# Layer 0's cross-attention: key norms spread through a row in DRAM, maxima of the two halves exchanged by two DMAs from ScalarE

## The reference, cut to what matters

```python
xn = layernorm(x, ln_x_g, ln_x_b)
ln = layernorm(latents, ln_l_g, ln_l_b)
q = (ln @ Wq).reshape(b, m, h, d).transpose(0, 2, 1, 3)
kv = jnp.concatenate([xn @ Wkv, ln @ Wkv], axis=1)
...
qn = rmsnorm(q, qn_g) * scale
kn = rmsnorm(k, kn_g)
sim = jnp.einsum('bhid,bhjd->bhij', qn, kn)
...
attn = jax.nn.softmax(sim.astype(jnp.float32), axis=-1).astype(sim.dtype)
out = jnp.einsum('bhij,bhjd->bhid', attn, v)
out = out.transpose(0, 2, 1, 3).reshape(b, m, h * d)
return out @ Wout + bout
```

## Time and profile before

| | us |
|---|---|
| median of 3 runs | 3336.15 |
| lowest and highest | 3332.85, 3337.33 |
| the profiled execution | 3327.6 |
| its span | 3325.8 |
| steps of the stage, first `shift` to last | 122.4 to 1313.0 |
| TensorE busy, whole span | 2892.9 (87%) |
| VectorE, ScalarE, GpSimd busy | 1606.0, 1071.9, 508.3 |

### The profile page before, as it was taken

One profiled execution on the slowest core, in us unless ns is written; L12 is line 12 of the kernel. 1 busy time (PEld: TensorE's weight loads), 2 busy tenths in 40 slices (PEclk: granted clock), 3 DMA queues, 4 the chain that ended last, 5 costly groups with the idle time before them and its releaser, 6 DMA issues. The chain is left out here.

```text
span 3325.8 us, 44201 instructions
## 1 busy us (share of the span) xinstructions
PE 2892.9 (87%) x17968; PEld 1930.7 (58%) x17968; DVE 1606.0 (48%) x3626; ACT 1071.9 (32%) x1925; POOL 508.3 (15%) x280
## 2 busy tenths in 40 slices
PE   4899999999999999779999978998965789688776
PEld 2465656666665666445555635666942459577644
DVE  4445454545555443535555546764531340355564
ACT  2232323333333322114445536532321423111121
POOL 2011120202020200000000004761010130243200
PEclk8899999999999999889999989998987889899898
DMA  4000000000000000121010001115857149423001
GB/s 135 0 1 22 1 23 6 18 23 1 23 1 23 1 1 1 71 106 41 21 41 21 1 6 33 45 41 203 320 195 229 50 163 324 146 86 113 32 1 32
DMA packets 80704, 215.92 MB, mean 65 GB/s; under 512 B 5232, under 2 KB 53896, under 8 KB 73848
## 3 DMA queue, kind: packets, MB, share of 16 engines
q1 hardware_dynamic: 77528, 204.98, 18.2%
q0 software_dynamic: 2976, 8.13, 0.7%
HBM read 201.99 MB, written 10.58 MB: 64 GB/s over the span
## 5 line engine op out<-in xcount | busy, mean ns | idle before, releaser
L1339 PE MATMUL L_xattn_bank<-L_xattn_keys_tok,L_xattn_probsT 119*128 119x257 f32 (+1 forms) x1792 | 437.6, 389 | 1.4 <-ACT L_xattn_probsT L1172 1.4
L1273 PE MATMUL L_xattn_wide<-L_xattn_keys_feat,weights_a 128*128 128x512 f32 (+2 forms) x1024 | 388.1, 523 | 3.0 <-DVE L_xattn_max L1008 1.3
L1339 PEld LDWEIGHTS L_xattn_bank<-L_xattn_keys_tok,L_xattn_probsT 119*128 119x128 f32 (+1 forms) x1792 | 324.3, 189 | 112.3 <-ACT L_xattn_probsT L1172 42.6
L1166 ACT ACTIVATE L_xattn_scores<-L_xattn_scores,L_xattn_neg_max 128x833 f32<-128x833 f32 x128 | 119.7, 983 | 627.7 <-DVE L_xattn_neg_max L1013 627.7
L1273 PEld LDWEIGHTS L_xattn_wide<-L_xattn_keys_feat,weights_a 128*128 128x128 f32 x1024 | 190.6, 192 | 157.7 <-issue 128.7
L2280 DVE TENSOR_TENSOR_SCAN L_attn_state<-L_attn_decay,L_attn_banks 128x1024 f32<-128x1024 f32 x80 | 182.7, 2286 | 69.6 <-PE L_attn_banks L2483 61.6
L998 DVE TENSOR_TENSOR L_xattn_k_normed<-L_xattn_wide,L_xattn_k_normed 128x834 f32<-128x834 f32 x128 | 125.4, 1021 | 172.8 <-PE L_xattn_wide L1287 172.8
L1555 DVE CUSTOM_DVE_ANT_0 L_xattn_scores<-L_xattn_banks,L_xattn_mask 128x512 f32<-128x512 f32 (+1 forms) x256 | 131.5, 570 | 151.8 <-issue 151.8
L1093 POOL TENSOR_TENSOR L_xattn_keys_tok<-L_xattn_keys_tok,weights_a 119x1792 f32<-119x1792 f32 (+2 forms) x24 | 61.1, 2545 | 938.4 <-DVE L_xattn_keys_tok L933 938.4
L2386 POOL TENSOR_TENSOR L_attn_state<-L_attn_state,L_attn_C_rows 128x1024 f32<-128x1024 f32 x80 | 188.7, 2360 | 70.3 <-DVE L_attn_state L2280 70.2
L1008 DVE CUSTOM_DVE_ANT_0 L_xattn_scores<-L_xattn_wide,L_xattn_mask_row 128x833 f32<-128x833 f32 x128 | 126.4, 1021 | 129.4 <-issue 129.4
(11 more groups left out here) (506 smaller groups left out, 4590.8 us busy)
## 6 DMA issues: line engine op xcount, KB each, us to landing
L_xattn_ctx_feat<-in_ctx_feat SPq DMA_DIRECT2D x24, 1601.0 KB, 10.2
L_ffn_expert_w<-in_x_L_ffn SPq DMA_DIRECT2D x16, 2056.0 KB, 8.4
L_ffn_expert_w<-in_x_L_ffn SPq DMA_DIRECT2D x15, 1028.0 KB, 6.0
L_ffn_expert_w<-in_x_L_ffn SPq DMA_DIRECT2D x15, 1024.0 KB, 5.6
L_xattn_keys_tok<-in_ctx_tok SPq DMA_DIRECT2D x8, 1547.0 KB
L_attn_C_rows<-L_attn_c_rows SPq DMA_DIRECT2D x48, 256.0 KB, 3.2
L_xattn_ctx_tok<-in_ctx_tok SPq DMA_DIRECT2D x8, 1536.0 KB
L_xattn_ctx_tok_and_one<-in_ctx_tok SPq DMA_DIRECT2D x8, 1536.0 KB
```

The source lines that it names most:

```text
L1273: last = nc.tensor.matmul(wide[:, 2 * h + c, 0:n], wk[:, k, p * P:(p + 1) * P], xnT[b % 2][:, k, a:a + n], start=(k == 0), stop=(k == KT - 1))
L1339: last = nc.tensor.matmul(bS[:, 0:D + 1], pT[0:r, c, a, :, :].rearrange("p h q -> p (h q)"), xn[b % 2][0:r, t, :], start=(t == 0), stop=(t ...
```

## The change

1. `spread` on TensorE is gone. ScalarE stores the norms of a step as rows into a small DRAM tensor `k_scale_rows` (two DMAs, four rows of 417 numbers each), and SyncE loads them back, each row broadcast to 64 partitions (two DMAs of 64 x 1668 numbers, 427 KB each), into the SBUF tile `spread`. `keys_normed` reads that tile, one iteration later than before, and `scores` waits for the clamp of step s + 1 in place of its product.
2. `swap_max` on TensorE is gone. ScalarE issues two DMAs of 64 x 2 numbers that move each half's maxima to the partitions of the other (`other`); `shift` becomes a maximum and a negation and moves into the iteration of its own scores, as do the exponentials.
3. TensorE's order: transposes of groups 0 and 1 between the two halves of the keys, groups 2 and 3 after them, the mix cut into 4, 2 and 8 tiles in place of 5, 5 and 4 (in an order that takes the tiles of ScalarE's copies first), `apply_v` behind the scores.
4. SyncE loads the tokens of a context as 112 and 7 partitions in place of 119, and from batch 2 on behind the norms' load of step p = 1. VectorE's statistics come after `shift`.

```diff
+    EVEN = 112
...
+    MIX_ORDER = [(c, a) for part in (range(4), range(4, HALF_T)) for c in range(2) for a in part]
...
+        spread = sb("k_scale", [P, 4, QK])
+        k_scale_rows = nc.dram_tensor(name + "k_scale_rows", (2, 2, KP), F32, kind="Internal").ap()
...
+        other = sb("max_of_other_half", [P, 2])
...
+                near = (TILES - 1) * TR
+
+                def load_ctx(b):
                     if b >= 2:
                         sp.wait_ge(mixed, NQ * (b - 1))
-                    near = (TILES - 1) * TR
                     rows = L.aps["ctx_tok"][b]
-                    sp.dma_start(xn[b % 2][0:TR, 0:TILES - 1, 0:D], rows[0:near, :].rearrange("(t p) d -> p t d", p=TR)
-                                 ).then_inc(ctx_loaded[b % 2], 16)
+                    far = rows[0:near, :].rearrange("(t p) d -> p t d", p=TR)
+                    for a, c in ((0, EVEN), (EVEN, TR)):
+                        sp.dma_start(xn[b % 2][a:c, 0:TILES - 1, 0:D], far[a:c]).then_inc(ctx_loaded[b % 2], 16)
...
+                def move_latents(b):
+                    sp.dma_start(xn[b % 2][NEAR:NEAR + S, TILES - 1, 0:D], L.z[(b % 2) * S:(b % 2 + 1) * S, b // 2, :]
+                                 ).then_inc(latents_moved[b % 2], 16)
+
+                def spread_scale(s):
+                    sp.wait_ge(k_scale_stored, 32 * (s + 1))
+                    if s >= 1:
+                        sp.wait_ge(kn_ready, 2 * s)
+                    for h in range(2):
+                        sp.dma_start(spread[h * DH:(h + 1) * DH, :, :].rearrange("p j n -> p (j n)"),
+                                     k_scale_rows[s % 2, h:h + 1, :].broadcast_to([DH, KP])).then_inc(k_scale_moved, 16)
+
+                load_ctx(0)
+                load_mask(0)
+                sp.wait_ge(latents_ready, 1)
+                for b in range(2):
+                    move_latents(b)
+                load_ctx(1)
+                load_mask(1)
+                for s in range(STEPS):
+                    b, p = divmod(s, NQ)
+                    spread_scale(s)
+                    if p == 1 and 1 <= b < B - 1:
+                        load_ctx(b + 1)
+                        move_latents(b + 1)
+                        load_mask(b + 1)
+
...
                     if piece == 0:
-                        dve.wait_ge(ctx_loaded[b % 2], 32 * (b // 2) + 32)
+                        dve.wait_ge(ctx_loaded[b % 2], 48 * (b // 2) + 48)
...
                 def keys_normed(s):
-                    dve.wait_ge(k_spread, s + 1)
+                    dve.wait_ge(k_scale_moved, 32 * (s + 1))
                     for x in range(2):
                         k = kn[:, s % 2, 2 * x * QK:2 * (x + 1) * QK].rearrange("p (a n) -> p a n", n=QK)
-                        nc.vector.tensor_tensor(k, wide[:, 2 * x:2 * x + 2, 0:QK], k, ALU.mult).then_inc(kn_ready, 1)
...
-                    dve.wait_ge(swapped, s + 1)
-                    nc.vector.scalar_tensor_tensor(nm[:, :], mx[:, :], -1.0, bO[:, 320:322], ALU.mult, ALU.min
-                                                   ).then_inc(shifted, 1)
+                    dve.wait_ge(swapped, 32 * (s + 1))
+                    chain(nc.vector.tensor_tensor(mx[:, :], mx[:, :], other[:, :], ALU.max))
...
-                    if behind:
-                        shift(s - 1)
                     if ahead:
                         key_copy(s + 1, 0)
+                    if behind:
+                        weights_turned(s - 1, 1)
+                    if ahead:
                         key_copy(s + 1, 1)
                     if behind:
-                        weights_turned(s - 1, 1)
                         weights_turned(s - 1, 3)
+                    if s < STEPS:
+                        keys_normed(s)
                     if ahead:
                         key_clamp(s + 1)
-                    if ahead:
-                        keys_normed(s + 1)
-                    if s >= 2:
-                        keep_result(s - 2)
                     if turns:
                         keys_turned(b + 1, p - 5, 0)
                     if s < STEPS:
                         score_max(s)
-                        if turns:
-                            keys_turned(b + 1, p - 5, 1)
-                        if b + 1 < B:
-                            if p == 1:
-                                ctx_stats(b + 1, 0)
-                            if p == 2:
-                                ctx_stats(b + 1, 1)
-                                ctx_norm(b + 1, 0)
-                            if p == 3:
-                                ctx_norm(b + 1, 1)
+                    if s >= 2:
+                        keep_result(s - 2)
+                    if s < STEPS:
+                        shift(s)
+                    if turns:
+                        keys_turned(b + 1, p - 5, 1)
+                    if s < STEPS and b + 1 < B:
+                        if p == 1:
+                            ctx_stats(b + 1, 0)
+                        if p == 2:
+                            ctx_stats(b + 1, 1)
+                            ctx_norm(b + 1, 0)
+                        if p == 3:
+                            ctx_norm(b + 1, 1)
...
+                    act.wait_ge(k_rnorm, 2 * s + 2)
+                    if s >= 2:
+                        act.wait_ge(k_scale_moved, 32 * (s - 1))
+                    for h in range(2):
+                        nc.scalar.dma_start(k_scale_rows[s % 2, h].rearrange("(j n) -> j n", n=QK), rk[h:P:32, :]
+                                            ).then_inc(k_scale_stored, 16)
+
+                def swap_max(s):
+                    act.wait_ge(s_taken, 2 * s + 2)
+                    if s >= 1:
+                        act.wait_ge(shifted, s)
+                    for c in range(2):
+                        nc.scalar.dma_start(other[(1 - c) * S:(2 - c) * S, :], mx[c * S:(c + 1) * S, :]).then_inc(swapped, 16)
...
                     if behind:
-                        exponentials(s - 1)
+                        weights_turned(s - 1, 0)
                     if ahead:
                         key_square(s + 1, 0)
                     if behind:
-                        weights_turned(s - 1, 0)
+                        weights_turned(s - 1, 2)
                     if ahead:
                         key_square(s + 1, 1)
-                    if behind:
-                        weights_turned(s - 1, 2)
                     if s >= 2:
                         mixed_turned(s - 2)
                     if ahead:
@@ -1208,6 +1253,9 @@
                     if turns:
                         keys_turned(b + 1, p - 5, 0)
                         keys_turned(b + 1, p - 5, 1)
+                    if s < STEPS:
+                        swap_max(s)
+                        exponentials(s)
...
-                    elif s:
+                    if s == 1 and h == 0:
+                        pe.wait_ge(k_clamped, 1)
+                    if s >= 2:
                         pe.wait_ge(s_taken, 2 * (s - 2) + h + 1)
...
-                def spread(s):
-                    pe.wait_ge(k_rnorm, 2 * s + 2)
-                    for j in range(4):
-                        last = nc.tensor.matmul(wide[:, j, 0:QK], L.const[32 * j:32 * (j + 1), C_SPREAD:C_SPREAD + P],
-                                                rk[32 * j:32 * (j + 1), :], start=True, stop=True)
-                    last.then_inc(k_spread, 1)
...
                     b, p = divmod(s, NQ)
-                    pe.wait_ge(kn_ready, 2 * min(s + 1, STEPS - 1) + 2)
-                    if s + 1 == STEPS:
+                    pe.wait_ge(kn_ready, 2 * s + 2)
+                    if s + 1 < STEPS:
+                        pe.wait_ge(k_clamped, s + 2)
...
-                    pe.wait_ge(s_taken, 2 * s + 2)
-                    if s >= 2:
-                        pe.wait_ge(att_ready, s - 1)
-                    nc.tensor.matmul(bO[:, 320:322], L.const[:, C_SWAP:C_SWAP + P], mx[:, :], start=True, stop=True
-                                     ).then_inc(swapped, 1)
-
...
-                        pe.wait_ge(pT_odd, 2 * s + 2)
                         if s >= 1:
                             pe.wait_ge(oh_ready, s)
-                    for t in tiles:
+                    if tiles[0] == 4:
+                        pe.wait_ge(pT_odd, 2 * s + 2)
...
                     pe.wait_ge(oh_ready, s + 1)
```

46 lines of the change are left out of this document (19 added, 27 removed).

## The result

The changed kernel takes 3488.57 us (median of 4 runs, 3478.69 to 3492.07) against 3334.5 (3332.34 to 3337.33) on the same chip: ratio 1.0457, 95% interval 1.0434 to 1.048. It is 154 us **slower**; 3270 was forecast, with 3228 to 3345 as the range.

What follows compares the result with a forecast made beforehand. TensorE's queue was taken as the bound; -74 + 25 - 6 - 9 = -64 gave 3263.6 from 3327.6 us, and with the runs' 8.5 us offset, rounded down, 3270 us. Range 3228 to 3345 us.

Steps and rivals of the forecast that it cites:

- the exchange, now a transfer: Maxima moved by two small ScalarE DMAs: landing L 3.3 us beside the norms' stream, stall 0.4 us a step, +25 us.
- Rival B: Exchange waits for the whole queued stream: L 4.4 us, stall 1.5 us, +93 instead of +25, 3340 us; chance 0.13.
- Rival C: Exchange lands like 128 KB transfers, L 5.7 us; TensorE stalls 2.8 us before each step's transposes; 3421 us; chance 0.11.
- Matmuls out of the step: TensorE's queue loses spread, exchange and a wait: -1.20 us a step, plain step 17.16, -74 us over 62 steps.
- The norms' round trip: Norms through DRAM land with 6 us of cover before VectorE's product; product reading SBUF within 0.2 us, covered; cost 0.
- Rival A: Exchange hidden, L under 2.9 us: no stall, and the statistics' 10 us gained; 3237 us; chance 0.32.
- Loading context 0: At the start, loading 112 and 7 partitions instead of 119 shortens VectorE's wait: -6 us, bounds 0 and -12.9.
- Ramp: Keys of step 1 and scores of step 0 start earlier, needing only clamps: -9 us, bounds -4 and -9.
- Statistics behind: VectorE's context statistics placed after the wait for the exchange: 2.6 us late in step 2, against 2.5 before; cost 0.

Runs made afterwards that it cites:

- experiment 9: Changed kernel, norms' loads issued three ways: four DMAs of 417 columns each, 3316.55 us; destination padded into short rows, 3531.5; second load after the first landed, 3328.19.
- the padded run: Changed kernel with the loads' destination padded by a column, so each partition gets four rows of 1668 bytes: 3531.5 us, ratio 1.0577.
- experiment 8: Changed kernel with 20, then 10, added matmuls filling TensorE's wait before the first transposes: 3564.44 us, then 3478.17 us.
- experiment 1: Changed kernel with SyncE issuing the norms' loads only when the exchange of the step before has landed: 3268.32 us, ratio 0.9805.
- experiment 6: experiment 1 with GpSimd's gain and bias done tile by tile: 3223.33 us, ratio 0.9667; the same edit in the kernel before: 3327.71 us.

## Why the prediction was wrong

**The step that failed** is *the exchange, now a transfer*: "If it shares each engine evenly with the stream it lands at the latest as the stream ends, L = 3.4. I take 3.3". There is no even sharing. L is 5.2 us and an issue 0.53 instead of 0.35; the stall was put at 0.4 us a step, +25, and is about 2.6 (19.62, the shortest plain step, less 17.01), over 62 steps +162. The end of the stream was also set too early, at S + 7.5: a 427 KB load takes 5.4 us here, and the second is issued near S + 3.6.

*The rivals.* Rival B had the right mechanism, waiting for everything queued, and the Trainium skill's packet rule beside it ("DMA: Bandwidth & Descriptors", on queues, rings and completion order). The changed kernel agrees with that rule, experiment 9 only in part: each load of the padded run has 16 rows an engine, 32 in both, more than the 9 to 17 after which the rule switches, and in the 25 steps with both loads ahead nearly everything still went first. B's price was off for the same reason as above, L = 4.4. Rival C had the sign, the place (`turn_weights(s, 0)`) and nearly the size, 2.8 us a step; it got 0.11. The row of 5.7 us was the only one of small transfers beside a stream, and I argued it away by the stream's size.

*A term that was missing.* The wait's effect on the clock. The sum priced a stall at its length; in a plain step in which the clock fell it costs some 1.5 us more (experiment 8). Of the 223 us between the stages of the changed kernel and of experiment 1, 66 are matmuls that ran slower, at 0.95 against 0.99 in the mean. C's 3421 comes within 68 us of 3489 without this term, but also without the products' loss and the stops told below, so that the two sizes are alike is partly luck.

*Matmuls out of the step*, -1.20 and a plain step of 17.16: right, 17.01 once the exchange is out of the way, and the wait before the first tile of the mix, read as forecast (from the mixed tokens' two transposes, less 0.23), is 0.29 us in the median (0.24 forecast).

*The norms' round trip*, 0 for its landing: right, 1.9 us of waiting in all. But "the product reads SBUF where it read PSUM; both bounds within 0.2 us, covered too" failed: beside GpSimd it takes up to 4.54 us. With what by-tile gains change in the ramp it was worth 45 us in experiment 1 (3268 to 3223), which is why Rival A's 3237 was missed there and beaten in experiment 6. In the changed kernel it is part of the third steps' 25.2 us. The prediction did not weigh this neighbour of the new operand.

*Loading context 0*, -6: the wait shrank by 6.1 us; made alone the edit gave 8.5, by its interval 5 to 15. *Ramp*, -9: together with the context -15, and the first scores start 11.5 us earlier, the first `shift` 11.3; in experiment 1 it is 16.4. *Statistics behind* `shift`, 0: off; in experiment 1 their place was worth 14 us.

*A second path through the exchange*, put at nothing. Once in a batch, in its seventh step, TensorE's queue stands still before the keys, and the profile names no releaser. VectorE's rows beside it and the kernel do:

```profile
417.61 0.16 DVE L1046 TENSOR_TENSOR L_xattn_max<-L_xattn_max,_xattn_max_of_other_half 128x2 f32<-128x2 f32 x1 [4.88 <-DMA _xattn_max_of_other_half<-L_xattn_max]
...
417.88 0.40 DVE L1016 COPY L_xattn_keys_feat<-L_xattn_bank 128x237 f32<-128x237 f32 x1
...
418.38 4.73 PE L1321 MATMUL L_xattn_wide<-L_xattn_keys_feat,weights_a 128*128 128x512 f32 x8 [3.21 <-issue]
```

These keys are the first of the next batch, and `keys` waits (`xT_dve`) for VectorE's last copy of the turned tokens, `keys_turned(b + 1, 1, 1)`. The change moved that copy behind `shift`, and so behind the exchange. In all seven batches the keys start 0.10 us after the copy has ended. The seven stops of 3.1 to 3.6 us make the group's 23.1 us, and the keys behind this one run at a clock of 0.63 (418.38 to 423.00 us). The same group has 3.9 in experiment 1, 4.2 with a quarter of the stream, 9.6 and 12.9 with the loads one after the other and in quarters, 27.2 with short rows: it goes with the landing of the exchange. In these steps the transposes then have no wait of their own, so the stops add less than their length. No run puts the copy back ahead of `shift`.

## What to carry to other kernels

A small transfer on ScalarE's queue took 1.8 us with nothing ahead of it, and otherwise had to wait for what SyncE had issued before it: order big loads behind it with a wait, and count its latency to the end of what is queued. When work moves behind a wait, look at everything that moves with it: here a copy for the next batch did. Before an operand moves from PSUM to SBUF, look at what GpSimd runs beside it. And a stall of 2.5 us in every step on TensorE cost more than its length in about half of the plain steps.
